# Window attention and 3x3 convolution: tokens in one 32-bit copy in patch order, single 32-bit matmuls for q, k and v, and a shorter Newton iteration

## The reference

```
x = x + window_attention(group_norm(x))   # 8x8 windows of 7x7 tokens, 8 heads of 16, shifted by 3 pixels
x = x + conv3x3(group_norm(x))            # weights scale*sign(w) - clip(w) + clip(w), times a mask

window_attention: qkv = tokens @ Wqkv.T + b ; q *= 16**-0.5
                  attn = softmax(q k^T + relative_bias + mask) ; (attn @ v) @ Wproj.T + b
group_norm: 32 groups of 4 channels, (x - mean) / sqrt(var + 1e-5) over all pixels of the group
```

## Time and profile before

| what | value |
|---|---|
| median of three runs | 3491.44 us |
| the profiled execution's own time | 3491.2 us |
| its span, first to last instruction | 3489.4 us |
| busy: PE, PEld, DVE, ACT, POOL | 92%, 77%, 83%, 70%, 66% |
| mean granted TensorE clock | 0.981 of full |
| first and last subtraction on POOL (L435) | 86 us and 3413 us |

### The profile page before, as it was taken

How to read it: one execution, slowest core, us unless ns; L and a number is a source line. 1 busy time by engine, 2 the same in 40 slices (tenths; PEclk the granted TensorE clock), 3 DMA queues, 4 the chain that set the end, 5 groups by cost and what they waited for, 6 DMA issues and landing times.

```text
span 3489.4 us, 154043 instructions
## 1 busy us (share of the span) xinstructions
PE 3214.1 (92%) x64139; PEld 2700.3 (77%) x64139; DVE 2902.3 (83%) x6143; ACT 2450.3 (70%) x5473; POOL 2295.0 (66%) x3683
## 2 busy tenths in 40 slices
PE   2899999999999999999999999999999999999996
PEld 1678778778878778878778878778878778788785
DVE  5688888888888888888888888888888888888885
ACT  1777777777767777777777767777767777777772
POOL 4476666776666776666766666766667766657764
PEclk9999999999999999999999999999999999999998
DMA  2112211222211222211222211222111222112111
GB/s 59 37 45 53 49 43 48 51 51 53 50 41 48 51 51 53 51 40 48 52 49 53 49 41 48 49 52 52 45 45 47 51 52 50 43 45 51 33 36 36
DMA packets 352643, 165.99 MB, mean 48 GB/s; under 512 B 148048, under 2 KB 351952, under 8 KB 351952
## 3 DMA queue, kind: packets, MB, share of 16 engines
q1 hardware_dynamic: 351952, 156.13, 18.4%
HBM read 53.31 MB, written 51.38 MB: 30 GB/s over the span
## 4 chain that ended last, share of the span: by engine, by line
PE 58%; DVE 17%; POOL 12%; issue 9%; ACT 2%; SPq 1%; DMA 0%; DVEq 0%; POOLq 0%; ACTq 0%
PE conv_ps L997 15%; PE qkv_ps L879 11%; PE scores_ps L892 8%; PE probsT_ps L903 7%; PE attn_ps L916 5%; PE attn_ps L920 4%; PE misc_ps L968 4%; DVE s_sb L750 4%; DVE plane_lo L762 3%; POOL s_sb L435 3%; PE misc_ps L959 2%; DVE s_max L755 2%; PE misc_ps L965 2%; POOL plane L462 2%; POOL gn_t L419 1%
## 5 line engine op out<-in xcount | busy, mean ns | idle before, releaser
L435 POOL TENSOR_TENSOR s_sb<-s_sb,s_max 113x392 f32<-113x392 f32 x1024 | 959.6, 937 | 1019.5 <-DVE s_max L755 1018.8
L497 ACT COPY probsT<-probsT_ps 128x392 f32<-128x392 f32 x1024 | 495.1, 483 | 365.6 <-PE probsT_ps L903 348.7
L490 ACT ACTIVATE probs<-s_sb 113x392 f32<-113x392 f32 x1024 | 553.2, 540 | 174.6 <-POOL s_sb L435 172.1
L462 POOL TENSOR_TENSOR plane<-x_n 128x224 f32<-128x224 f32 x896 | 640.7, 735 | 18.7
L903 PE MATMUL probsT_ps<-ident,probs 113*128 113x113 f32 x4096 | 587.8, 266 | 70.0 <-ACT probsT L497 70.0
L755 DVE TENSOR_REDUCE s_max<-s_sb 113x8 f32<-113x392 f32 x1024 | 574.5, 561 | 35.2
L750 DVE TENSOR_TENSOR s_sb<-scores_ps,bias 113x392 f32<-113x392 f32 x1024 | 565.7, 552 | 36.7 <-PE scores_ps L892 29.8
L558 ACT COPY v<-qkv_ps 64x256 f32<-64x256 f32 (+2 forms) x1280 | 390.2, 324 | 217.9 <-PE qkv_ps L879 211.9
L903 PEld LDWEIGHTS probsT_ps<-ident,probs 113*128 113x128 f32 x4096 | 434.6, 142 | 125.8 <-ACT probs L490 84.3
L997 PE MATMUL conv_ps<-plane_hi,wc_hi 128*128 128x224 f16 x2688 | 487.1, 264 | 24.4 <-DVE conv_y L824 20.3
L997 PE MATMUL conv_ps<-plane_hi,wc_lo 128*128 128x224 f16 x2688 | 480.6, 262 | 0.0
(11 more groups left out here) (138 smaller groups left out, 6364.6 us busy)
## 6 DMA issues: line engine op xcount, KB each, us to landing
x_in<-in_x_dram SPq DMA_DIRECT2D x224, 224.0 KB, 3.1
recip_wide<-recip SPq DMA_DIRECT2D x1024, 49.0 KB
out_dram<-x_out SPq DMA_DIRECT2D x224, 224.0 KB, 2.3
x<-in_L_conv_w_dram SPq DMA_DIRECT2D x1, 576.0 KB
x<-L_conv_pruning_mask_dram SPq DMA_DIRECT2D x1, 576.0 KB
x_n<-_conv_rel_pos_table_dram SPq DMA_DIRECT2D x14, 10.7 KB
x_n<-in_mask_dram SPq DMA_DIRECT2D x1, 196.0 KB
plane<-n_L_conv_qkv_weight_dram SPq DMA_DIRECT2D x1, 192.0 KB
```

Source lines behind the costliest of these rows:

```text
L435: nc.gpsimd.tensor_tensor(s, s, top, ALU.subtract).then_inc(sub_ready, 1)
L462: last = nc.gpsimd.tensor_tensor(plane[:, t % 2, j], *sums[j])
L490: nc.scalar.activation(probs[0:QP, slot % 2, :, :, 0:N], s_sb[0:QP, slot % 4], ACT.Exp)\
L497: nc.scalar.copy(probsT[:, g % PT_SLOTS], probsT_ps[:].rearrange("p (w n) -> p w n", n=ODD)[:, :, 0:N])\
```

## The change

- The two 16-bit token arrays become one 32-bit array `tokens` in patch order, 49 to a window. POOL writes it directly at the places where it wrote `x_n`; ACT's and DVE's passes over the tokens are gone, and with them their semaphores. A row now takes three pieces on POOL (seven whole windows, and two parts of the window that the shift cuts), the last row six. A wait on `qkv_ready` is added before each row.
- q and k: one 32-bit matmul of 392 columns each. v: for each of 8 windows two 32-bit matmuls with the window's 49 tokens as weights and 64 columns moving, even heads on column tile 0 and odd heads on column tile 64; all of it at j = 2, nothing at j = 3.
- v leaves PSUM in two copies of 49 partitions by 512 elements.
- Newton: seven `tensor_scalar` instructions that take their factors from memory, in place of 14 `tensor_tensor`.
- The memsets of the 16-bit tokens and one weight rounding in the setup are gone. `x_n` is used by the convolution alone, so two waits before it is written are gone.

```diff
-NORM1_AT, HI_AT, LO_AT = 23, 24, 26
+NORM1_AT = 23
+def patch_pieces(row0):
+    whole, rest = divmod(WRAP, WIN)
+    for rows, cols, y0, x0 in roll_pieces(WIN, row0):
+        if cols.start == 0:
+            yield rows, slice(0, whole), slice(0, WIN), y0, x0
+            yield rows, slice(whole, NWIN), slice(0, rest), y0, x0 + whole * WIN
+        else:
+            yield rows, slice(whole, NWIN), slice(rest, WIN), y0, x0
...
-                    then(tt(gn.t[:], gn.y[:], gn.y[:], ALU.mult))
-                    then(tt(gn.t[:], gn.t[:], gn.half[:], ALU.mult))
-                    then(tt(gn.t[:], gn.t[:], three_halves[:], ALU.add))
-                    then(tt(gn.y[:], gn.t[:], gn.y[:], ALU.mult))
-                then(tt(gn.shift[:], gn.kept_out[:], gn.mean[:], ALU.subtract))
-                tt(gn.shift[:], gn.shift[:], gn.y[:], ALU.mult).then_inc(gn.ready, 1)
+                    then(ts(gn.t[:], gn.y[:], gn.y[:], gn.half[:], ALU.mult, ALU.mult))
+                    then(ts(gn.y[:], gn.t[:], three_halves[:], gn.y[:], ALU.add, ALU.mult))
+                ts(gn.shift[:], gn.kept_out[:], gn.mean[:], gn.y[:], ALU.subtract, ALU.mult).then_inc(gn.ready, 1)
...
-                        for rows, cols, y0, x0 in roll_pieces(WIN, row * WIN):
-                            n, m = rows.stop - rows.start, cols.stop - cols.start
-                            rows = slice(1 + row * WIN + rows.start, 1 + row * WIN + rows.stop)
-                            last = nc.gpsimd.tensor_scalar(x_n[:, rows, cols], x_of[(i + 1) % 3][:, y0:y0 + n, x0:x0 + m],
-                                                           gn1.y[:], gn1.shift[:], ALU.mult, ALU.add)
+                        need(pool, qkv_ready, (i * ROWS + row + 1) * QKV_JOBS)
+                        patches = tokens[:, row * NWIN:(row + 1) * NWIN, :].rearrange("p w (r c) -> p w r c", c=WIN)
+                        for rows, wins, cols, y0, x0 in patch_pieces(row * WIN):
+                            n, m, width = rows.stop - rows.start, wins.stop - wins.start, cols.stop - cols.start
+                            last = nc.gpsimd.tensor_scalar(
+                                patches[:, wins, rows, cols],
+                                x_of[(i + 1) % 3][:, y0:y0 + n, x0:x0 + m * width].rearrange("p r (w c) -> p w r c", c=width),
+                                gn1.y[:], gn1.shift[:], ALU.mult, ALU.add)
...
-                            parts = ([(0, 4, 0, 0), (0, 4, 1, 1)] if j == 2 else
-                                     [(0, 4, 4, 0), (0, 3, 5, 1), (3, 1, 0, 1)])
...
+                            vals = qkv_ps[:].rearrange("p (w a d) -> p w a d", w=NWIN, d=HD)
+                            for e in range(2):
+                                half = slice(ODD * e, ODD * e + N)
+                                last = nc.scalar.copy(v[half, slot, :, :, e * HD:(e + 1) * HD], vals[half])
...
-                        nc.scalar.copy(
-                            tok_hi[:, row * NWIN:(row + 1) * NWIN, 0:N].rearrange("p w (r c) -> p w r c", c=WIN),
...
-                        vec.tensor_tensor(
-                            tok_lo[:, at, 0:N].rearrange("p w (r c) -> p w r c", c=WIN),
...
                 if j < 2:
-                    hi, lo = tok_hi[:, wins, 0:N], tok_lo[:, wins, 0:N]
-                    last = three(qkv_ps[:, 0:RT].rearrange("p (w n) -> p w n", n=N),
-                                 ((wT_hi[:, j, :], hi), (wT_hi[:, j, :], lo), (wT_lo[:, j, :], hi)))
+                    last = mm(qkv_ps[:, 0:RT], wT[:, j, :], tokens[:, first:first + NWIN, :].rearrange("p w n -> p (w n)"),
+                              start=True, stop=True)
                 else:
-                    runs = [(b * C, slice(0, 128), (j - 2) * 4 + b) for b in range(4)]
...
+                    weights = wT[:, 2, :].rearrange("p (a e d) -> p a e d", e=2, d=HD)
+                    for w, e in product(range(NWIN), range(2)):
+                        last = mm(qkv_ps[ODD * e:ODD * e + N, w * ODD:(w + 1) * ODD], tokens[:, first + w, :],
+                                  weights[:, :, e, :], start=True, stop=True)
...
-                    if live(i, 0 if u // PAIRS < ROWS - 1 else 1):
+                    if u % PAIRS < QKV_JOBS and live(i, 0 if u // PAIRS < ROWS - 1 else 1):
                         qkv(i, u)
```

More of the change, by code:

```diff
@@ L208, in build_block @@
         x_n = sb("x_n", [128, H + 2, W])
-        tok_hi = sb("tok_hi", [128, ROWS * NWIN, ODD], F16)
-        tok_lo = sb("tok_lo", [128, ROWS * NWIN, ODD], F16)
+        tokens = sb("tokens", [128, ROWS * NWIN, N])
         plane = sb("plane", [128, 2, PLANES, TPAIRS, W])
@@ L384, in _ @@
         def _(pool):
-            for buf in (tok_hi, tok_lo, plane_hi, plane_lo):
+            for buf in (plane_hi, plane_lo):
                 last = nc.gpsimd.memset(buf[:], 0.0)
@@ L407, in newton @@
             def newton(gn, img):
-                tt = nc.gpsimd.tensor_tensor
+                ts = nc.gpsimd.tensor_scalar
                 done = [0]
@@ L539, in body @@
                     r, j = divmod(u, PAIRS)
-                    if live(i, 0 if r < ROWS - 1 else 1):
-                        number, slot = (i * ROWS + (r + 1)) * 4 + j, (r + 1) % 2
+                    if j < QKV_JOBS and live(i, 0 if r < ROWS - 1 else 1):
+                        number, slot = (i * ROWS + (r + 1)) * QKV_JOBS + j, (r + 1) % 2
                         act.wait_ge(qkv_ready, number + 1)
-                        tokens = qkv_ps[:, 0:RT].rearrange("p (w n) -> p w n", n=N)
+                        sums = qkv_ps[:, 0:RT].rearrange("p (w n) -> p w n", n=N)
@@ L545, in body @@
                         if j == 0:
-                            last = nc.scalar.activation(q[:, slot], tokens, ACT.Identity, bias=q_bias[:], scale=q_scale[:])
+                            last = nc.scalar.activation(q[:, slot], sums, ACT.Identity, bias=q_bias[:], scale=q_scale[:])
                         elif j == 1:
                             for e in range(2):
-                                last = nc.scalar.activation(k[:, slot, :, e, :], tokens, ACT.Identity,
+                                last = nc.scalar.activation(k[:, slot, :, e, :], sums, ACT.Identity,
@@ L873, in _ @@
             pe.wait_ge(scales_ready, 1)
-            def three(out_ps, pairs_of_parts):
-                for n, (w, t) in enumerate(pairs_of_parts):
-                    last = mm(out_ps, w, t, start=(n == 0), stop=(n == 2))
-                return last
             def scores(i, u):
@@ L911, in values @@
                 pe.wait_ge(probsT_sb, (row + 1) * PAIRS)
-                pe.wait_ge(qkv_free, (row + 1) * 4)
+                pe.wait_ge(qkv_free, (row + 1) * QKV_JOBS)
                 need(pe, o_ready, row)
@@ L928, in qkv @@
                 row = (r + 1) % ROWS
-                number = (i * ROWS + (r + 1)) * 4 + j
+                number = (i * ROWS + (r + 1)) * QKV_JOBS + j
                 need(pe, qkv_free, number)
                 if j == 0:
-                    pe.wait_ge(tok_lo_ready, i * ROWS + (r + 1) + 1)
-                wins = slice(row * NWIN, (row + 1) * NWIN)
+                    pe.wait_ge(gn1.applied, i * ROWS + (r + 1) + 1)
+                first = row * NWIN
                 if j < 2:
-                    hi, lo = tok_hi[:, wins, 0:N], tok_lo[:, wins, 0:N]
-                    last = three(qkv_ps[:, 0:RT].rearrange("p (w n) -> p w n", n=N),
-                                 ((wT_hi[:, j, :], hi), (wT_hi[:, j, :], lo), (wT_lo[:, j, :], hi)))
-                else:
-                    runs = [(b * C, slice(0, 128), (j - 2) * 4 + b) for b in range(4)]
-                    if j == 3:
-                        runs[3:] = [(3 * C, slice(0, ODD), NWIN - 1), (3 * C, slice(ODD, 128), 0)]
-                    for col, parts, w in runs:
-                        at, width = (row * NWIN + w) * ODD, parts.stop - parts.start
-                        hi, lo = (t[:].rearrange("p w n -> p (w n)")[:, at:at + width] for t in (tok_hi, tok_lo))
-                        last = three(qkv_ps[parts, col:col + C],
-                                     ((hi, wT_hi[:, 2, :]), (lo, wT_hi[:, 2, :]), (hi, wT_lo[:, 2, :])))
+                    last = mm(qkv_ps[:, 0:RT], wT[:, j, :], tokens[:, first:first + NWIN, :].rearrange("p w n -> p (w n)"),
+                              start=True, stop=True)
+                else:
+                    weights = wT[:, 2, :].rearrange("p (a e d) -> p a e d", e=2, d=HD)
+                    for w, e in product(range(NWIN), range(2)):
+                        last = mm(qkv_ps[ODD * e:ODD * e + N, w * ODD:(w + 1) * ODD], tokens[:, first + w, :],
+                                  weights[:, :, e, :], start=True, stop=True)
                 last.then_inc(qkv_ready, 1)
```

33 lines of the change are left out of this document (5 added, 28 removed).

## The result

The changed kernel takes 3440.6 us in the median of four runs (3435.2 to 3450.6), the kernel before 3489.7 beside it. The ratio is 0.9863 with a 95% interval of 0.9833 to 0.9892: 1.4% faster. The forecast was 3347 us; of the 144 us foreseen, 49 came.

A forecast was written before the change was run, and what follows sets the result against it. PE, 92% busy, was taken as the bound, with its own work and standstills counting. Terms -0.7 + 0.4 - 0.75 - 1.95 - 1.4 = -4.4 us an image, x 32 = -141, and -3 once: -144, so 3347 us; range 3285 to 3460.

The forecast's parts named there:

- q and k: PE's projections: a 32-bit pair holds PE about 0.69 us against 0.51 for three 16-bit matmuls, +0.36 a row.
- v after: PE at j = 2, two column tiles side by side: 1.10 us, -0.47 a row; with q and k, -0.11 a row.
- Stall at u = 24 and clock: PE's 2.15 us wait at the values goes, -1.95 us an image; the clock's fall after it too, -1.4.
- The clock should stay up: With no such standstill at u = 24, the fall to 1.2 GHz stays away: -1.4 us an image, bounds 0 and -1.6.
- Stall at u = 8 to 12: PE's waits on POOL's chain shrink by Newton's 0.75 us an image; PE's losses at q, k, v are hidden or regained.
- ACT: ACT's v copies at j = 2 come later and last longer, delaying its next tasks: +0.4 us an image, bounds 0 and 2.4.
- Normalised rows: On POOL, three pieces in place of two add 0.36, so 1.4 us a row; 2.4 for the last.
- Newton's instructions: On POOL, seven instructions take 2.9 us: -0.75 at u = 8 and, stretched, -1.0 at u = 23.
- DVE's lost pass: DVE loses `tok_lo`, 8 passes an image of about 0.7 us; nothing counted for it.
- the POOL one: Patch writes cost twice on the long piece, so POOL becomes the bound at u = 24 to 31: 3456; chance 0.20.
- the third: Column tiles don't run beside each other in 32 bits, or weight loads hold them up; v 2.0 us a row: 3539; chance 0.10.
- The fourth: The clock still falls and ACT's late copies make new waits: 3417 us; chance 0.15.

The follow-up runs named there:

- v_at_3: The changed kernel with all of v's matmuls and copies at j = 3 in place of j = 2: 3438.4 us.
- the moved pass alone: The kernel before with only ACT's `tok_hi` pass over row 0 moved from the end of unit 24 to the end of unit 25: 3429.6 us, ratio 0.9848.
- qk_short: The changed kernel with q and k matmuls over only the first 300 of a row's 392 tokens: 3420.0 us.

## Why the prediction was wrong

The change gave 1.90 us an image where I had 4.4. By stretch, foreseen with the row's -0.11 put where PE was taken to be the bound:

```
                                        foreseen   measured
units 4 to 15, no fall                    -0.86      -0.09
units 24 to 27, no fall                   -2.06      -1.48
the other rows, no fall                   -0.04      +0.59
longer stands that only some images have    -        +0.5
the clock's falls                         -1.4       -1.40
```

The first three are medians of images without a fall, the fourth is their mean less that. The ends of the program gave almost nothing: images 2 and 30 each hold a longer fall after and none before, and took 3.5 and 2.0 us more; only the head gave 5.3 us where I had 3.

*q and k* (+0.36 a row): 7.48 less 7.16 is +0.32. Right.

*v after* (1.10 us, -0.47 a row): the instructions take 1.03 and the change into column tiles 0.09, so 1.12, as forecast; the tiles do run beside each other. But units 2 and 3 show only -0.33 (median). The old v ended on column tiles right ahead of the scores, which are on tiles too, and one change of 0.10 did for both; now the convolution stands between, and the scores pay their own 0.09 again. `v_at_3`, with v back ahead of the scores, gets 0.11 back. The row is 12.07 us after 12.08, not -0.11. The term was missing a third change of tiling: 0.7 us an image, all that it was to give.

*Stall at u = 24 and clock* (-1.95 and -1.4): units 24 to 27 gave 3.18 us, foreseen as 3.35. Of these 1.75 are the falls that are gone from there (24 in all before), the rest is the stall (1.48 by the medians). The wait at the values did go. What I had too short was the normalisation of row 0 behind Newton: 1.78 us, not 1.4. Newton alone takes 0.5 of the stall away, the moved pass alone 0.9, both together 1.4; for the falls each of the two is enough.

*The clock should stay up*: half right, and the -1.4 came out by luck. The falls cost more than I took (1.79 us an image: a shorter kind costs 1.5 and a longer kind 3.2), and 0.39 came back in another place, 8 of them at unit 12. I had counted on "no such standstill" and not asked where PE would next stand: at the transposes of unit 12, for 1.50 us, since v's second half no longer fills unit 11.

*Stall at u = 8 to 12* (-0.75): this is the step whose mechanism failed. Newton did give 0.65 there (from the subtraction of unit 8 to that of unit 13: 15.07 us before, 14.42 after, by the table of events). I wrote that what PE loses at q, k and v beside POOL's chain is hidden. The chain begins earlier than I placed it, at PE's hand-over of the second norm in units 6 and 7, so q and k of units 4 and 5 lie ahead of it, +0.32, and those of units 12 and 13 behind it, +0.25; `qk_short` gives both back. v's saving lies inside it, where it is worth nothing. Unit 14's scores start at 31.80 after 31.87, so of 0.86 foreseen for units 4 to 15 less than 0.1 came, and then the clock's falls come on top: the means are 38.43 us against 38.05. This is 0.8 of the 2.5 us an image that are missing. I priced a change of PE's work by its sum over a row, when the parts that grew were on the path and the part that shrank was not.

*ACT* (+0.4, bound 2.4): units 14 to 31 carry new waits for ACT's copy of x, for DVE's drain and at the transposes (at full clock the rows beside the two stalls are 0.6 us longer than before). v in two steps takes 0.9 us an image back (103.25 to 102.35), of which 0.7 is not the clock. So this term was about two times too small.

*Normalised rows, Newton's instructions, DVE's lost pass*: as forecast (1.34 to 1.36 us for three pieces, row 0 apart; 3.0 us for Newton at unit 8 and 3.7 at unit 23; nothing).

Of the rivals, the POOL one is refuted: writing in patches shows no cost (343 elements 0.752 us). So is the third: v takes 1.12 us and not 2.0. The fourth, that the clock still falls and ACT's late copies make new waits, is what happened, at 3441 where I had 3417; I gave it 0.15.

## What to carry to other kernels

An engine busy 92% is not the bound in every stretch: take one steady image apart at fixed marks, find the stretches in which another engine runs without a gap, and price each moved or resized piece by the stretch that it falls in, hand-overs in the busy engine's list included. Try the cheap part of a change alone: here a shorter scalar chain and one reordered pass, at 3379 us, gave 3.5% where the change with its rebuilt matmuls gave 1.4%. When a wait that brings the clock down is removed, look for the next longest one.

## What the runs showed of the hardware

A change of the array's tiling costs PE about 0.09 us, seen as a later start of the instruction behind it: v's first matmul starts 0.19 us after a convolution matmul (1609.15 to 1609.34), where another convolution matmul starts after 0.10. On two column tiles 32 matmuls in 32 bits start within 1.03 us, although each of their weight loads takes 0.124. On POOL a one-column `tensor_scalar` with two factors in memory takes 0.34 us, a `tensor_tensor` 0.19, so halving the number of instructions saves 0.64 us of 3.6 and not half. Of the 1.0 us saved at unit 23, half was lost again, since the same normalisation took 1.50 us when it started earlier and 1.02 when it started later. A fall of the clock to 1.2 GHz costs an image about 1.5 us in its shorter kind and 3.2 in its longer one (106.55 against 103.36 before); matmuls whose results nobody reads, put into PE's wait, kept the clock up in all 27 images that had one.
